# Projection weights and the first context in one input array and one transfer

## What is computed

```python
Q = (ctx @ Wq.T);  K = (ctx @ Wk.T)              # Wq, Wk are 64 x 64
sim = Q @ K.T / (sqrt(16) * 4)                   # 256 x 256, all heads summed
keep the 76 largest of every row of sim          # k = int(256 * 0.3)
A = sigmoid(sim) * kept;  A = (A + A.T) / 2
x = x + (1 - gamma) * layernorm(x) + gamma * A
z = layernorm(x)
x = x + shared_ffn(z) + sum over the 2 best of 8 experts of weight * expert_ffn(z)
```

## Time and profile before

| | |
|---|---|
| Three runs, median | 113.53 us (113.2 to 114.8) |
| Profiled execution, first to last instruction (span) | 111.5 us |
| TensorE busy in it | 102.9 us, 92% |
| Landing of batch 0's context, after an issue at 0.72 | 2.3 us |
| Landing of the projection weights, after an issue at 0.73 | 2.6 us |
| First weight load of `project(0)` | 3.41 us |

### The profile page before, as it was taken

How to read it: one execution, slowest core, us unless ns; L and a number is a source line. 1 busy time by engine, 2 the same in 40 slices (tenths; PEclk the granted TensorE clock), 3 DMA queues, 4 the chain that set the end, 5 groups by cost and what they waited for, 6 DMA issues and landing times.

```text
span 111.5 us, 2502 instructions
## 1 busy us (share of the span) xinstructions
PE 102.9 (92%) x816; PEld 100.5 (90%) x816; DVE 84.4 (76%) x276; ACT 61.7 (55%) x155; POOL 70.4 (63%) x141
## 2 busy tenths in 40 slices
PE   6899709889999999999999999999999999999990
PEld 6699608778999999999999999999999999999990
DVE  6689899899998789867659979759418979365731
ACT  4179999989669856289691245243513352052400
POOL 4047788894975887899898591697028550465500
PEclk9999997699999999999999999999999999999999
DMA  2699995000003700000029000010483004520002
GB/s 40 135 341 370 343 374 163 3 0 3 0 0 96 281 9 0 3 0 6 3 47 309 21 9 0 32 62 0 111 263 104 6 3 154 228 94 0 0 0 94
DMA packets 8158, 10.33 MB, mean 93 GB/s; under 512 B 1936, under 2 KB 6544, under 8 KB 8144
## 3 DMA queue, kind: packets, MB, share of 16 engines
q1 hardware_dynamic: 7776, 10.13, 28.6%
q10 hardware_dynamic: 368, 0.04, 0.3%
HBM read 9.09 MB, written 1.08 MB: 91 GB/s over the span
## 4 chain that ended last, share of the span: by engine, by line
PE 78%; POOL 8%; DVE 5%; ACT 4%; issue 2%; POOLq 0%
PE ps_h L1407 23%; PE ps_u L1407 22%; PE ps_y L1435 20%; PE ps_a L1435 3%; PE ps_c L1354 3%; PE ps_u L1280 3%; ACT qkT L577 2%; PE ps_b L1337 1%; DVE near L970 1%; PE ps_a L1325 1%; PE ps_h L1289 1%; POOL rs L371 1%; DVE st L870 1%; DVE left L962 1%; DVE z L1060 1%
## 5 line engine op out<-in xcount | busy, mean ns | idle before, releaser
L452 POOL TENSOR_TENSOR gc<-prod,weights 128x512 f32<-128x512 f32 x16 | 25.9, 1634 | 15.3 <-DMA weights<-gates 9.3
L699 ACT ACTIVATE sil<-ps_h 128x512 f32<-128x512 f32 (+1 forms) x20 | 10.9, 552 | 16.1 <-PE ps_h L1407 16.1
L710 ACT ACTIVATE g_hi<-gc 128x512 fp32r<-128x512 f32 x16 | 10.1, 630 | 15.9 <-POOL gc L452 15.9
L1435 PE MATMUL ps_y<-dn_hi,g_hi 128*128 128x256 f32 x63 | 17.9, 284 | 0.0
L1435 PE MATMUL ps_y<-dn_hi,g_lo 128*128 128x256 f32 x63 | 17.7, 281 | 0.0
L1435 PE MATMUL ps_y<-dn_lo,g_hi 128*128 128x256 f32 x63 | 17.7, 281 | 0.0
L1136 DVE TENSOR_TENSOR g_lo<-gc,g_hi 128x512 fp32r<-128x512 f32 x16 | 13.8, 862 | 2.5 <-ACT g_hi L710 2.1
L1407 PE MATMUL ps_h<-z_hi,up_hi 128*128 128x256 f32 x70 | 14.7, 291 | 0.0
L1124 DVE TENSOR_TENSOR prod<-sil,ps_u 128x512 f32<-128x512 f32 x16 | 10.8, 679 | 4.9 <-ACT sil L699 3.2
L1407 PE MATMUL ps_h<-z_hi,up_lo 128*128 128x256 f32 x70 | 14.0, 281 | 0.0
L1407 PE MATMUL ps_u<-z_hi,up_hi 128*128 128x256 f32 x70 | 14.0, 281 | 0.0
(11 more groups left out here) (210 smaller groups left out, 250.3 us busy)
## 6 DMA issues: line engine op xcount, KB each, us to landing
weights<-gates SPq DMA_DIRECT2D x8, 512.0 KB, 4.5
x_sb<-in_x SPq DMA_DIRECT2D x4, 256.0 KB, 6.0
up_raw<-in_w1t SPq DMA_DIRECT2D x4, 256.0 KB, 5.9
up_raw<-in_w3t SPq DMA_DIRECT2D x4, 256.0 KB, 6.0
dn_raw<-in_w2t SPq DMA_DIRECT2D x4, 256.0 KB, 6.2
out_x<-fin SPq DMA_DIRECT2D x3, 256.0 KB, 2.1
out_x<-fin SPq DMA_DIRECT2D x2, 128.0 KB, 1.7
ctx_sb<-in_ctxT SPq DMA_DIRECT2D x1, 192.0 KB, 4.6
```

What stands on the lines that cost most here:

```text
L452: nc.gpsimd.tensor_tensor(gc[k % 2][:, :].rearrange("p (n t q) -> p n t q", n=2, t=T), prod[s][:, :].rearrange("p (n t q) -> p n t q", n=2 ...
L699: nc.scalar.activation(sil[i % 2][:, :w], ps_h[i % 2][:, :w], ACT.Silu).then_inc(silu_ready, 1)
L710: nc.scalar.activation(g_hi[s][:, :], src[:, :], ACT.Copy).then_inc(ghi0_ready if s == 0 else ghi_ready, 1)
L1435: last = nc.tensor.matmul(dst[:, t * D:(t + 1) * D], g[s][:, tok], w[:, e, :], start=(s == 0 and first and m == 0), stop=(s == SLOTS - 1 a ...
```

## The change

The input arrays `wqkT` and the batch 0 part of `ctxT` become one array, `firstT`: each of its 64 rows holds 64 values of Wq, 64 of Wk and the 256 of batch 0's context, 1536 bytes in a row. SP brings it as its first transfer into one tile, `first_sb`. ScalarE's transfer of the weights is gone, and so is one of VectorE's memsets, since one tile has its lower rows zeroed in place of two. TensorE waits for 16 on a semaphore of this transfer alone. The context of batches 1 to 3 has its own array and tile; its transfer is as large as before and stays second on SP.

```diff
-        ctx_sb = sb("ctx_sb", [P, B * N])
-        wqk_sb = sb("wqk_sb", [P, 2, DC])
+        first_sb = sb("first_sb", [P, 2 * DC + N])
+        ctx_sb = sb("ctx_sb", [P, LAST * N])
...
         def _(sp):
-            sp.dma_start(ctx_sb[0:DC, 0:N], ctxT[:, 0:N]).then_inc(ctx0_in, 16)
-            sp.dma_start(ctx_sb[0:DC, N:], ctxT[:, N:]).then_inc(ctx_in, 16)
+            sp.dma_start(first_sb[0:DC, :], firstT).then_inc(first_in, 16)
+            sp.dma_start(ctx_sb[0:DC, :], ctxT).then_inc(ctx_in, 16)
...
         def _(act):
-            act.dma_start(wqk_sb[0:DC, :, :], wqkT).then_inc(ctx0_in, 16)
             nc.scalar.preload_act_table(ACT.Silu)
...
             def zero_rows():
-                nc.vector.memset(wqk_sb[DC:P, :, :], 0.0)
-                nc.vector.memset(ctx_sb[DC:P, 0:N], 0.0)
+                nc.vector.memset(first_sb[DC:P, :], 0.0)
                 nc.vector.memset(qkT[0][DC:P, :, :], 0.0).then_inc(rows_ready, 1)
-                nc.vector.memset(ctx_sb[DC:P, N:], 0.0)
+                nc.vector.memset(ctx_sb[DC:P, :], 0.0)
...
                 if b == 0:
                     pe.wait_ge(rows_ready, 1)
-                    pe.wait_ge(ctx0_in, 32)
+                    pe.wait_ge(first_in, 16)
+                    ctx = first_sb[:, 2 * DC:]
                 else:
                     pe.wait_ge(rows_ready, 2)
                     pe.wait_ge(ctx_in, 16)
-                nc.tensor.matmul(ps_qk[b][:, 0:N], wqk_sb[:, :, :].rearrange("p a c -> p (a c)"),
-                                 ctx_sb[:, b * N:(b + 1) * N], start=True, stop=True).then_inc(qk_ready, 1)
+                    ctx = ctx_sb[:, (b - 1) * N:b * N]
+                nc.tensor.matmul(ps_qk[b][:, 0:N], first_sb[:, 0:2 * DC], ctx,
+                                 start=True, stop=True).then_inc(qk_ready, 1)
...
-        "ctxT": f["ctx_512"].transpose(2, 0, 1).reshape(DC, B * N),
-        "wqkT": np.stack([f["L0_xattn_Wq"].T, f["L0_xattn_Wk"].T], axis=1),
+        "firstT": np.concatenate([f["L0_xattn_Wq"].T, f["L0_xattn_Wk"].T, f["ctx_512"][0].T], axis=1),
+        "ctxT": f["ctx_512"][1:].transpose(2, 0, 1).reshape(DC, LAST * N),
```

More of the change, by code:

```diff
@@ L43, in experts_of, with attention_ffn @@
     return [0] if slot == 0 else [2 * slot - 1, 2 * slot]
-def attention_ffn(nc, x, ctxT, wqkT, gamma, gateT, w1t, w3t, w2t, ws1t, ws3t, ws2t, out):
+def attention_ffn(nc, x, firstT, ctxT, gamma, gateT, w1t, w3t, w2t, ws1t, ws3t, ws2t, out):
     es = ExitStack()
@@ L185, in attention_ffn @@
         ps_sim = [None, ps_b, ps_h[0], ps_h[1]]
-        ctx0_in = sem("ctx0_in")
+        first_in = sem("first_in")
         ctx_in = sem("ctx_in")
```

## The result

The kernel became slower: 115.75 us (median of 4 runs, 115.53 to 115.85) against 113.42 us (4 runs, 113.2 to 114.8). The ratio is 1.0187, with a 95% interval of 1.013 to 1.0244: it is slower, and whether by more than 2% these runs leave open. The span of the profiled execution went from 111.5 to 113.9 us. The forecast was 0.1 us faster, in a range that ended at 114.5.

What follows compares the result with a forecast made beforehand. TensorE's unbroken work from 28 us was taken as the bound, so only a shift of its start counts. Landing 0.18 us sooner, halved by the clock to 0.09, other terms nothing: 113.53 - 0.1 = 113.4 us, range 113.0 to 114.5.

Steps and rivals of the forecast that it cites:

- What bounds the kernel: TensorE is busy without a gap from 28 to 105 us; a start change is worth the shift reaching 28 us.
- The landing: First transfer, 96 KB issued at 0.72, lands at 3.15; project(0)'s weight load at 3.23, 0.18 us sooner than 3.41.
- the worst bound of 2.88: Straight line through SP's 64 KB and 192 KB transfers: 2.88 us for 96 KB, landing at 3.60, costing +0.13 us.
- The doubled rate that I gave to longer rows: The first transfer's 32 KB more take 0.23 us at 142 GB/s, 0.11 at twice that; 0.13 was taken.
- The argument that a second transfer costs something of its own: At the start, two landings lie 0.3 us apart though issued 0.01 apart; held against the landing staying put.
- Rival 2: First transfer lands later, after 3.33, from longer rows and gamma issued sooner; at 3.60 +0.13 us, 113.7; chance 0.15.
- The clock: TensorE rises from 1.2 to 2.4 GHz at 4.25, during project(0), and the rise stays there after the change.
- The halved price of a shift: Work moved before 4.25 runs at half speed, so 0.18 us sooner is worth 0.09 us at project(0)'s end.
- Does it reach 28 us: VectorE's 0.31 and batch 0 x's 0.14 us of room let the 0.09 us gain through; ScalarE shifts with project(0).
- The rule: Transfers from different issuers share 16 DMA engines, so the first landing stays at 3.33 and the change is 0.
- rival 3: TensorE's half-clock period moves from 17.9-21.3 us onto busy work at 24.6-28.0: +1.4 us, 114.8; chance 0.10.
- All three signs that I had named against the prediction: First landing past 3.33, clock rise moving with project(0), or low clock anywhere but between 17 and 22 us.

Runs made afterwards that it cites:

- small transfers late: The merged kernel with gamma and the gate weights issued by SP behind x of batch 1, not by ScalarE at the start: 113.33 us, ratio 0.997.
- gate weights first: The merged kernel with only the gate weights issued by ScalarE at the start and gamma issued by SP behind x of batch 1: 113.56 us, ratio 0.9994.

## Why the prediction was wrong

**What bounds the kernel.** Right. The start is worth what it shifts the unbroken work of TensorE, and 2.41 us of shift at 26 us became 2.4 us of span.

**The landing.** Wrong in this kernel, right as a sum of its own. I had 2.43 from issue to landing, 3.15; it was 3.4, beyond even the worst bound of 2.88. With the broadcast of gamma out of the way it was 2.3 to 2.7 in the profiles of five kernels, inside the bounds from the bytes, and 3.3 in that of a sixth. The doubled rate that I gave to longer rows did not show: 150 GB/s in the stretch with late small transfers, for 142. The argument that a second transfer costs something of its own, since the weights came 0.3 behind the context, does not stand: with late small transfers the context came 0.3 behind the weights.

**The step that failed: "ScalarE's table load and its two small transfers are issued some 0.6 us sooner; nobody waits for them, and I cost them at nothing."** That nobody waits for a transfer says nothing of what it does to those beside it. Before, gamma's issue followed that of the weights, and it landed 4.7 us after its issue at 1.36, at 6.1. With the weights' issue deleted it landed at 3.45 (2.7 after 0.75), ahead of the first transfer, and 26 packets of ScalarE's queue were under way before 2.0 us, when SP's queue had none (with 128 addresses it was 38, so to be ahead is not enough). The runs showed +0.78 us on the load of project(0) in place of nothing, and with the clock behind it +2.41 at 26 us. Rival 2 named this shift, but priced it by bytes in a straight line, +0.13 at most, where half a kilobyte from one address halved the rate of the engines, 73 GB/s for 142.

**The clock.** The halved price of a shift was derived from the assumption that the rise stays at 4.25, since TensorE "starts those at 0.98 in both kernels". I looked at where the activity began and not at what may break it off. In the merged kernel TensorE's streams stopped for 0.74 us ahead of project(0), and the rise came at 9.2. In the kernel before, two warm-ups fewer cost 1.1 us with nothing landing later. So the later landing was not worth half its delay, as I had it, but three times: 2.41 for 0.78. To give the slower side the factor of the faster side was the second mistake. With seven warm-ups, where the streams go on up to project(0), a load 0.84 later cost 0.45 in the median, and there the half fits.

**Does it reach 28 us.** Right: x of batch 0, the memsets and VectorE's idle times did not come into it. ScalarE carried the shift.

**The rule, and the rivals.** The rule of the Trainium skill, DMA: Bandwidth & Descriptors, section "Issuing engines are not separate DMA queues", that issuers share the 16 DMA engines, was cited for a change of 0. The landing it would have kept at 3.33 came at 4.1. That transfers of two issuers interleave, the merged kernel's trace bears out: packets of both queues stand in the same 0.8 us, 40 and 141. The low clock of rival 3 stayed where it costs nothing in the merged kernel's profile: 0.50 from 19.5 to 22.9, and TensorE still waits 0.92 us for the hits at 25.24. All three signs that I had named against the prediction came: a landing past 3.33, a rise that moved, and a low clock past 22 us.

## What to carry to other kernels

Deleting an issue moves up everything behind it on its queue; cost each of those against the transfers that it now runs beside, not by who waits for it. Where the start is a chain with warm-ups, let them reach the first real matmul even when its data is late: here two warm-ups fewer, which left 0.65 us open, cost 1.1 us. And do not broadcast a scalar from one address beside a transfer that matters; lay the copies out in the input, or issue it later.

## What the runs showed of the hardware

- 128 reads of 4 bytes from one address, issued 0.03 us after a 96 KB transfer on another queue, made it land after 3.3 to 3.4 us in place of 2.6, and the 16 engines moved 72 to 73 GB/s in place of 145. The same 128 packets from 128 addresses did not hold it up so.
- When TensorE came up from 1.2 to 2.4 GHz differed much between executions, with idle time ahead of project(0) and without. One profile each, the rise read from the distances of the passes:

| ahead of project(0) | kernels | rise at, us | span, us |
|---|---|---|---|
| five warm-ups, streams go on | 8 | 4.2 to 7.1 | 111.4 to 112.6 |
| seven warm-ups, streams go on, late load | 1 | 6.7 | 112.8 |
| three warm-ups, 0.65 us idle | 1 | 6.9 | 112.4 |
| five warm-ups, 0.56 and 0.66 us idle, late load | 2 | 7.5 | 113.1 |
| five warm-ups, 0.71 and 0.74 us idle, late load | 2 | 9.2 and 9.5 | 113.9 |

- So a late rise does not need an idle time. In two profiles with the load of project(0) at 3.15, the first statistics started at 5.68 and at 6.21; the first execution took 113.18 us and the second 114.10. The runs of the versions with five warm-ups and no early broadcast lie between 113.1 and 114.5, but for four (114.8 to 115.1); the four runs of the merged kernel lie within 0.3 us.

The two statistics, small transfers late and gate weights first:

```profile
5.68 0.43 DVE L868 BATCH_NORM_STATS2 st<-ps_c 128x6 f32<-128x256 f32 x1 [0.85 <-PE ps_c L1296]
```

```profile
6.21 0.43 DVE L868 BATCH_NORM_STATS2 st<-ps_c 128x6 f32<-128x256 f32 x1 [1.38 <-PE ps_c L1296]
```
